# Order of GpSimd's additions and of VectorE's aggregates around the second layer normalisation

## What is computed

```python
x = x + attention0(xn) + experts0(xn)
xn = _layernorm(x, axis=-1)          # (x - mean) / sqrt(var + 1e-5)
x = x + attention1(xn, ...) + ffn1(xn, ...)
# ffn1: h = xn * rsqrt(mean(xn*xn) + 1e-6) * norm_w
#       out = xn + routed(h) + shared(h)      <- xn itself is added to x
# attention1: 16 query heads in 4 groups over 4 key heads; the value of the output
#       needs the queries of a group summed: wqs = sum of 4 slices of Wq, bqs = sum of bq
```

## Time and profile before

| | |
|---|---|
| times of three runs | 1252.27 us median (1249.59 to 1254.02) |
| profiled execution | 1251.73 us, its span 1249.9 us |
| busy over the span | PE 1114.6 us (89%), DVE 793.5 (63%), ACT 559.2 (45%), POOL 566.6 (45%) |
| second normalising stage | about 849.1 to 875.8 us, between two barriers |
| granted TensorE clock | 0.943 on average |

### The profile page before, as it was taken

One profiled execution on the slowest core, in us unless ns is written; L12 is line 12 of the kernel. 1 busy time (PEld: TensorE's weight loads), 2 busy tenths in 40 slices (PEclk: granted clock), 3 DMA queues, 4 the chain that ended last, 5 costly groups with the idle time before them and its releaser, 6 DMA issues. The chain is left out here.

```text
span 1249.9 us, 21259 instructions
## 1 busy us (share of the span) xinstructions
PE 1114.6 (89%) x5586; PEld 837.5 (67%) x5586; DVE 793.5 (63%) x2450; ACT 559.2 (45%) x1488; POOL 566.6 (45%) x550
## 2 busy tenths in 40 slices
PE   5669999999996999959999999996888997999981
PEld 5446667777785889836666777785556765888861
DVE  5758877666504666649888677614954745666648
ACT  2226676555501444438777666713212332444420
POOL 0556777565400666654444343203276441555540
PEclk9779999999997999979999999998898997999985
DMA  9622222222146666532233223002569922555557
GB/s 333 258 77 86 95 94 90 74 76 75 39 190 175 181 182 185 162 110 85 85 94 78 83 65 84 30 1 80 199 213 300 291 86 83 164 166 166 164 171 246
DMA packets 113407, 169.17 MB, mean 135 GB/s; under 512 B 16975, under 2 KB 82734, under 8 KB 112766
## 3 DMA queue, kind: packets, MB, share of 16 engines
q1 hardware_dynamic: 95822, 123.46, 33.3%
q0 software_dynamic: 15296, 42.26, 9.3%
q10 hardware_dynamic: 2176, 2.10, 0.5%
HBM read 103.96 MB, written 63.80 MB: 134 GB/s over the span
## 5 line engine op out<-in xcount | busy, mean ns | idle before, releaser
L1339 POOL DMA_INDIRECT yk_dram<-work,place x143 | 137.8, 964 | 187.1 <-DVE place L1471 121.2
L1370 PE MATMUL bank<-big_a,probsT 128*128 x760 | 201.6, 361 | 0.4 <-DVE probsT L1442 0.4
L983 PE MATMUL bank<-kT,qT 128*128 128x256 f32 (+3 forms) x512 | 172.0, 458 | 0.0
L1094 DVE TENSOR_REDUCE negmax<-bank 128x1 f32<-128x256 f32 (+3 forms) x256 | 116.3, 487 | 68.3 <-PE bank L985 67.2
L1183 ACT ACTIVATE probs<-bank,negmax 128x256 f32<-128x256 f32 (+3 forms) x256 | 133.6, 531 | 51.4 <-DVE negmax L1094 50.1
L928 POOL TENSOR_TENSOR parts<-wq,parts 128x256 fp32r<-128x256 f32 x64 | 49.1, 766 | 225.6 <-ACT parts L1174 225.5
L1017 PE MATMUL bank<-probsT,big_b 128*128 128x512 f32 (+3 forms) x512 | 148.5, 433 | 0.0
L1370 PEld LDWEIGHTS bank<-big_a,probsT 128*128 128x128 f32 x760 | 130.8, 195 | 21.7 <-issue 2.5
L1001 PE MATMUL bank<-const,probs 128*128 128x128 f32 x640 | 128.6, 274 | 12.2 <-issue 5.7
L967 PE MATMUL bank<-parts 128*128 128x512 f32 x256 | 116.7, 491 | 21.1 <-POOL parts L928 16.4
L1203 ACT ACTIVATE probsT<-bank,kh 128x512 f32<-128x512 f32 (+3 forms) x256 | 120.4, 527 | 26.1 <-PE bank L1001 23.2
(11 more groups left out here) (230 smaller groups left out, 2232.1 us busy)
## 6 DMA issues: line engine op xcount, KB each, us to landing
probs<-xs_dram SPq DMA_DIRECT2D x190, 132.0 KB
work<-khT_dram SPq DMA_DIRECT2D x64, 256.0 KB, 3.3
xs_dram<-big_a SPq DMA_DIRECT2D x16, 792.0 KB, 11.1
wq<-in_wq SPq DMA_DIRECT2D x64, 128.0 KB, 2.3
big_a<-yk_dram SPq DMA_DIRECT2D x64, 128.0 KB, 2.1
big_a<-yk_dram SPq DMA_DIRECT2D x32, 256.0 KB, 6.5
big_a<-in_gu SPq DMA_DIRECT2D x1, 6144.0 KB, 18.2
stack_dram<-parts SPq DMA_DIRECT2D x24, 256.0 KB, 2.5
```

The lines of the kernel that those rows point to most:

```text
L983: nc.tensor.matmul(s.ps[bank][:, at:at + w], s.qT[:, par, i * P:(i + 1) * P], s.kT[:, par, 0:w], start=True, stop=False)
L1094: v.tensor_reduce(s.negmax[:, par, i:i + 1], s.ps[bank][:, at:at + (i + 1) * P], AX.X, ALU.max, negate=True).then_inc(maxed, 1)
L1339: nc.gpsimd.indirect_dma_start(out=d["yk"], out_offset=bass.IndirectOffsetOnAxis(ap=s.place[:, i % PLACES:i % PLACES + 1], axis=0), in_=ou ...
L1370: mm = nc.tensor.matmul(s.ps[2 + i % 2][:, 0:W], rowsT[:, i % 2, k * P:(k + 1) * P], gu[:, k, bass.ds(e * W, W)], start=k == 0, stop=k == ...
```

## The change

`statistics` aggregates each tile behind its own `bn_stats` group, and the loop of 16 at the end goes: twelve aggregates are issued with the first twelve `bn_stats`, one with each of the last four. In `norm_block1` GpSimd's four additions to x are issued first, each behind its wait for four normalised tiles, and the wait for the loads with the six sums comes after them. What is computed, all buffers and every other engine's program stay as they were.

```diff
@@ attention0, vector @@
         def statistics(tiles):
             for t in tiles:
                 v.bn_stats(s.stats[:, t, :], s.x[:, t, :]).then_inc(stat, 1)
+            for t in tiles:
+                dve.wait_ge(stat, t + 1)
+                v.bn_aggr(s.meanvar[:, t, :], s.stats[:, t, :]).then_inc(aggr, 1)
...
         if combining:
             dve.wait_ge(x_added, added_at["out", last, ROWS - 1])
             statistics([TILES - 1])
-            for t in range(TILES):
-                dve.wait_ge(stat, t + 1)
-                v.bn_aggr(s.meanvar[:, t, :], s.stats[:, t, :]).then_inc(aggr, 1)
@@ norm_block1, gpsimd @@
             add = nc.gpsimd.tensor_tensor
             link = Link(pool, plink)
 
+            for c in range(4):
+                pool.wait_ge(xn_ready, 4 * c + 4)
+                tiles = slice(4 * c, 4 * c + 4)
+                link(add(s.x[:, tiles], s.x[:, tiles], xn1[:, tiles], ALU.add))
             pool.wait_ge(attn_in, 16 * 10)
             link(add(wqs, raw_q[:, :, 0], raw_q[:, :, 1], ALU.add))
...
             link(add(bqs, bqs, bq[:, 3:4], ALU.add))
-            for c in range(4):
-                pool.wait_ge(xn_ready, 4 * c + 4)
-                tiles = slice(4 * c, 4 * c + 4)
-                link(add(s.x[:, tiles], s.x[:, tiles], xn1[:, tiles], ALU.add))
```

## The result

The changed kernel is slower: ratio 1.0075 against the kernel before (95% interval 1.006 to 1.0089; medians of 20 runs 1260.03 and 1252.16 us). Forecast were 5 us; the medians differ by 7.9, the ratio says 9.4. The profiled execution took 1261.32, span 1259.5. Ratios here leave out executions over 1.5% above the fastest of the same kernel; there was one, of r1.

The account below looks back on a forecast made before the run. The normalising stage, between barriers, lasts as long as its last engine, GpSimd alone for 5.1 us. Stage 6.0 longer, less 0.7, is 5.3 slower: from 1251.73 to 1257.0, by the median 1257.6; 1257.3 said, range 1250 to 1261.

Parts of the forecast that it names:

- Edit 1: End of the stage ahead: bn_aggr moved into VectorE's waits for TensorE gain 0.7 us, bounds 0 and 1.15.
- That GpSimd and VectorE hold each other up, L1576 among them, in turns: Normalising stage: GpSimd's additions and sums alternate with L1576 and L1584; last L1584 ends at 872.8 instead of 863.33.
- the second rival: Normalising stage: only L1584 is held up, L1576 not; 0.4 to 2.8 us slower, 1253.9 taken; chance 17%.
- the first rival: Normalising stage: no mutual hold-up, or VectorE keeps its turn; 5.8 us faster in all, 1246.2; chance 12%.
- These 3.35 us do 1.7 us of work: 1.65 us more. Bounds 0 and 3.: TensorE's continuous chain to the logits: 1.2 GHz until near 873 costs 1.65 us more, bounds 0 and 3.
- The third rival: The forecast's mechanism, with the next stage also late by 1.2 us through TensorE's clock: 1258.5; chance 5%.
- The cover of GpSimd's removed tail: End of the normalising stage: GpSimd's additions alone hold it 5.1 us, gained if the engines did not disturb each other.

Follow-up runs that it names:

- r1: The changed kernel unaltered, profiled a second time, against the kernel before: ratio 1.0043, stage 33.5 us.
- e6: The changed kernel without GpSimd's four additions of xn to x (output lacks them), against the kernel before: ratio 0.9936, stage 22.6 us.
- e4: The changed kernel with GpSimd's first addition held until VectorE has written four scaled tiles, against the kernel before: ratio 1.006, stage 37.7 us.
- e5: The changed kernel with GpSimd's first addition held until all 16 normalised tiles are written, against the kernel before: ratio 1.0089, stage 40.9 us.
- e1: The changed kernel with idle matmuls filling TensorE's waits in the normalising stage, against the kernel before: ratio 1.0012, stage 32.5 us.
- r3: The changed kernel unaltered, run a third time beside the filled version, against the kernel before: ratio 1.0059, stage 33.0 us.
- r2: Second run of the changed kernel with idle matmuls in TensorE's waits, against the kernel before: ratio 1.0003, stage 32.0 us.
- e3: Early aggregates; GpSimd's sums first, then two additions, the other two in its next program; against the kernel before: ratio 0.9959, stage 24.3 us.
- e7: Second run of the split version, two additions behind the sums and two in GpSimd's next program, against the kernel before: ratio 0.9949, stage 23.4 us.
- e2: Only the early aggregates, GpSimd's program as before, against the kernel before: ratio 0.9992, stage 27.84 us.
- e8: The changed kernel with the wait for the loads moved ahead of the additions; run once for its profile, no ratio, stage 27.85 us.

## Why the prediction was right or wrong

- **Edit 1.** Right: 0.65 for 0.7. (The sign given for it, the last bn_aggr ending 1.0 to 1.2 us behind the last bn_stats's start, was counted from the last but one: measured are 1.16 from that and 0.61 from the last.)
- **That GpSimd and VectorE hold each other up, L1576 among them, in turns.** Right, also in size: e6, without the additions, has none of the lateness. In the stage's own time the forecast had L1576 done at 13.66 us, the eighth L1584 at 20.4, the last at 23.6; measured were 13.66, 20.4 and 23.6. L1576 lasted 2.44 beside an addition, which rules the second rival out; the first rival is ruled out by the same rows. The inference from durations alone (0.41 for 256 columns with two per-partition scalars can't be the slow rate) carried it. Of the signs one was wrong beside a right working: a single L1584 takes over 1 us (2.58), not two to four; the three beside the sums take 0.86 to 0.94.
- **"These 3.35 us do 1.7 us of work: 1.65 us more. Bounds 0 and 3."** This term failed in size. It rested on "I expect 1.2 GHz until some 3 us into the continuous part, near 873". In the first profile, in e4 and in e5 TensorE kept 0.50 through 18.6 us and more of unbroken transposes and logits matmuls, and the term is 8.5 us against e1, far outside its bounds.

  In r1 and r3 the clock came back 4 us or so into the continuous part, near where it was forecast; there the term is 1.0 against e1 and r2, and the stage was 33.5 and 33.0 where 33.9 were said. The number told fits the faster heap, 1257.3 against its median of 1257.5.

  A case in which the clock doesn't come back I didn't have: I bounded its return by how it had come back in the earlier trace rows. The upper bound should have been the whole chain at half clock, 18.7 us in place of 9.85, which in place of the 1.65 gives 1264.5, near the slower heap's median of 1265.1. The same step put the logits 9 to 12 us later; in the first profile they are 18.4 later, counted from the stage's start. That the median of all, 1260.0, lies within 3 us of the forecast says nothing for this term: it falls between two heaps. What decides whether the clock comes back, with VectorE's and GpSimd's times equal to 0.01 us, no run here settles.
- **The third rival, 1.2 us lost in the next stage.** Not seen: from the next stage to the end the first profile of the change is 0.3 us longer, all told. Its condition, full clock at the next stage's start, wasn't met there (0.50 from 886.2 to 890.8), so this profile doesn't test the cost.
- **The cover of GpSimd's removed tail.** Right: 5.1 us were there, as e6 shows (5.3); e3 and e7 get 3.6 to 4.5 of it.

## What to carry to other kernels

Before moving a GpSimd operation under VectorE's work, read what VectorE issues there: beside L1584 (two inputs) or L1576 (one input at the fast rate) a GpSimd addition of 2.34 us let go by VectorE's own count cost VectorE 2.04 to 2.1 us, and beside MAX8 or FIND_INDEX8 nothing. When VectorE then feeds TensorE in short bursts, price the chain behind it at half clock throughout as the upper bound, not only its first microseconds. Give late work of the engine that ends the stage to the next stage's free stretch, as e3 and e7 do for 0.4 and 0.5%.

## What the runs showed that I had not expected

- A GpSimd operation that a DMA let go in the middle of back-to-back L1584 waited for the end of the stream, with VectorE at its normal length: 3.0 and 2.9 us in e3 and e7, 1.67 in e2, 1.1 in e6 for a sum of 0.64, 3.94 in e8 for an addition of 2.34. One that L1584's own count let go broke in at once (e4), and from then on they took turns. The moment within one L1584 doesn't separate them: in the five GpSimd's instruction starts 0.04 to 0.35 us behind the start of the L1584 in flight, in e4 0.16. Whether the releaser decides, or how much of the stream was left (1 to 5 tiles not yet begun in the five, 11 in e4), is open; neither was varied alone.
- Under unbroken transposes and logits matmuls the clock at 0.50 stayed there for 20 us or came back after 4, in the same program, and in e1 it fell from 1.00 to 0.50 under them.
